# Mixing the score products of one row tile with the maxima products of the other, and banks of two heads for half of the columns

## The reference

```python
att = jnp.einsum('bhtd,bhsd->bhts', q, k) / jnp.sqrt(jnp.asarray(D, x.dtype))
att = att + _alibi_causal_mask(T, H, x.dtype)[None]
att = jax.nn.softmax(att, axis=-1)
y = jnp.einsum('bhts,bhsd->bhtd', att, v)
...
h = jax.nn.silu(jnp.einsum('td,efd->tef', xf, w1))
y = jnp.einsum('tef,edf->ted', h, w2)
```

## Time and profile before

| | us |
|---|---|
| runs (3) | 578.05, 578.42 (median), 579.37 |
| span of the profiled execution | 575.7 |
| second group of heads (168.4 to 260.0) | 91.6 |
| third group of heads (260.0 to 351.6) | 91.6 |
| last group, with tasks (to 393.7), without (to 449.5) | 42.1, 55.8 |
| tile loop and end (449.5 to 575.7) | 126.2 |

### The profile page before, as it was taken

The page is one execution under the profiler, slowest core; times in us unless marked ns, Lnnn a source line. Parts: engine busy times, 40 slices in busy tenths (PEclk is TensorE's granted clock), DMA queues, the critical chain, the costliest instruction groups (busy, mean ns, idle before and its releaser), DMA issues.

```text
span 575.7 us, 15493 instructions
## 1 busy us (share of the span) xinstructions
PE 496.4 (86%) x5876; PEld 264.6 (46%) x5876; DVE 451.9 (79%) x775; ACT 400.9 (70%) x775; POOL 169.9 (30%) x293
## 2 busy tenths in 40 slices
PE   4756878889999999998999999989988999999970
PEld 2422323333243343333334325234433798999970
DVE  3689899989988998998998998995687555554451
ACT  4922366668888888888898887888788656555530
POOL 3310000010103102320034101047057860870864
PEclk9965599999999999999999999999899999999995
DMA  6592111000011450031310000010132222333332
GB/s 158 201 305 65 30 50 36 1 2 4 7 34 34 100 231 3 2 148 32 81 38 3 3 2 2 8 29 9 56 106 63 74 74 61 111 106 91 108 98 66
DMA packets 38263, 37.86 MB, mean 66 GB/s; under 512 B 7088, under 2 KB 33904, under 8 KB 37560
## 3 DMA queue, kind: packets, MB, share of 16 engines
q1 hardware_dynamic: 35808, 32.26, 19.5%
q0 software_dynamic: 2048, 4.20, 2.4%
q10 hardware_dynamic: 336, 0.42, 0.2%
HBM read 20.05 MB, written 16.61 MB: 64 GB/s over the span
## 4 chain that ended last, share of the span: by engine, by line
PE 59%; ACT 9%; DVE 5%; issue 3%; POOL 1%; DMA 1%; ACTq 0%; POOLq 0%; DVEq 0%
PE pv L745 18%; PE b L778 13%; PE b L852 8%; PE b L869 7%; ACT probs L1296 7%; PE b L717 6%; DVE part L1013 3%; PE b L692 3%; ACT raw L1266 1%; POOL raw L1478 1%; PE b L843 1%; PE b L647 1%; PE b L664 1%; ACT rows L1272 0%; DMA raw<-y_scratch,spots 0%
## 5 line engine op out<-in xcount | busy, mean ns | idle before, releaser
L1296 ACT ACTIVATE probs<-b 128x512 f32<-128x512 f32 (+1 forms) x576 | 298.6, 570 | 79.6 <-PE b L692 36.5
L1013 DVE TENSOR_REDUCE part<-b 128x2 f32<-128x1024 f32 (+2 forms) x320 | 327.7, 1061 | 26.8 <-PE b L717 11.8
L745 PE MATMUL pv<-probs,v_cur 128*32 128x256 f32 (+1 forms) x2432 | 176.7, 372 | 0.3 <-ACT probs L1296 0.2
L778 PE MATMUL b<-aug 55*128 55x512 bf16 (+3 forms) x640 | 114.2, 355 | 25.5 <-ACT probs L1296 21.3
L717 PE MATMUL b<-aug 52*128 52x512 bf16 (+3 forms) x640 | 117.1, 366 | 17.4 <-DVE part L1013 15.1
L778 PEld LDWEIGHTS b<-aug 55*128 55x128 bf16 x640 | 37.0, 93 | 137.6 <-ACT probs L1296 131.5
L745 PEld LDWEIGHTS pv<-probs,v_cur 128*32 128x32 f32 x2432 | 50.2, 109 | 68.3 <-issue 40.7
L852 PE MATMUL b<-hTt,inverse 128*128 128x128 f32 x424 | 56.3, 276 | 0.8 <-ACT hTt L1317 0.8
L869 PE MATMUL b<-w2T_sb,hst 128*128 x424 | 56.2, 276 | 0.8 <-ACT hst L1323 0.8
L869 PEld LDWEIGHTS b<-w2T_sb,hst 128*128 128x128 f32 x424 | 51.6, 192 | 1.2 <-issue 1.1
L852 PEld LDWEIGHTS b<-hTt,inverse 128*128 128x128 f32 x424 | 51.5, 192 | 1.0 <-issue 1.0
(11 more groups left out here) (151 smaller groups left out, 374.2 us busy)
## 6 DMA issues: line engine op xcount, KB each, us to landing
xt<-slot_scratch SPq DMA_DIRECT2D x53, 64.0 KB, 1.9
y_scratch<-aug SPq DMA_DIRECT2D x53, 64.0 KB, 1.5
slot_scratch<-slots SPq DMA_DIRECT2D x3, 1024.0 KB, 7.1
aug<-q_scratch SPq DMA_DIRECT2D x6, 384.0 KB
aug<-k_scratch SPq DMA_DIRECT2D x6, 384.0 KB
w2T_sb<-in_w2T SPq DMA_DIRECT2D x1, 2048.0 KB, 7.4
aug<-in_w1T SPq DMA_DIRECT2D x8, 256.0 KB, 2.6
q_scratch<-pieces SPq DMA_DIRECT2D x4, 384.0 KB, 2.6
```

What stands on the lines that cost most here:

```text
L745: return mm(pv[32 * hh:32 * hh + 32, c0:c1], v_cur[:, kb, hh, :], probs[:, step_ % 2, hh, at_:at_ + c1 - c0], start=(kb == 0 and c0 == 0), ...
L778: done.append(mm(pair[half][:, at_:at_ + w], k_aug[g % 2][n, b, kb * P:kb * P + P], q_aug[g % 2][n, b, (j + 1) * CW - w:(j + 1) * CW], sta ...
L1013: ins = nc.vector.tensor_reduce(dst, b1[:, slot:slot + 2, at_:at_ + w], AX.X, ALU.max)
L1296: nc.scalar.activation(probs[:, p % 2, hh, 0:w], b2[:, (n2 - 1) % RING2, 0:w], ACT.Exp).then_inc(exp_done, 1)
```

## The change

The three functions that issue products for a half step become generators that yield after each product, and a new function draws from two of them in turn, one per row tile.

- A bank of `b2` no longer holds one head's scores for all columns of the step, but two heads' (both pairs, one half) for half of the columns, the same half that the value products of that half step number take (`VALUE_PARTS[p][b]`). Each score product has half the columns, and there are twice as many.
- The banks are waited for one at a time, each ahead of its first product.
- The first task of pass 1 of a half step is mixed in: row tile 0 has the scores of half 0 and then the maxima of half 0; row tile 1 has the maxima of half 1 and then the scores of half 1. The two rows of products are issued alternately. Further tasks follow as before, and without a task both score rows alternate.
- Each bank signals ACT by itself. Value products wait only for the exps of their own half of the columns.
- ACT writes an exp's 512 results as two pieces of 256, one per pair.

```diff
-                def mask_out(pair, at_, table, cols):
+                def alternate(low, high):
 
-                    for h, (c0, c1) in enumerate(cols):
-                        for half in range(2):
-                            k = slice(HALF * half, HALF * half + HALF)
-                            ins = mm(pair[half][:, at_ + c0:at_ + c1], identh[k, h, :], table[k, h, c0:c1], start=False, stop=True, skip_group_check=True)
-                    return ins
+                    for _ in zip_longest(low, high):
+                        pass
...
+                def maxima(k, half, opens, closes):
...
+                    if opens:
+                        task_ready(k)
+                    at_ = 0
+                    for r in rs:
+                        w = (r + 1) * P if c == j else CW
+                        t = j * CW + r * P
+                        ins = mm(bank[:, at_:at_ + w], q_aug[buf][n, b, t:t + P], k_aug[buf][n, b, c * CW:c * CW + w], start=True, stop=True)
+                        if c == j:
+                            yield
+                            mask_out(bank, half, at_ + r * P, maskQ, 0, (0, P))
+                            yield
+                            ins = mask_out(bank, half, at_ + r * P, maskQ, 1, (HALF, P))
+                        if closes and r == rs[-1]:
+                            ins.then_inc(s1_ready, 1)
+                        yield
+                        at_ += w
...
+                    pe.wait_ge(exp_done, HG * (NSTEP * g_ + q) + 2 * (b + 1))
                     if b == 0:
-                        pe.wait_ge(exp_done, HG * (NSTEP * g_ + q + 1))
...
-                def scores(p, b):
+                def scores(p, b, half):
...
-                    for half in range(2):
-                        wait_slot(half)
-                    pair = [b2[:, (len(freed) + half) % RING2, :] for half in range(2)]
+                    n = slice(HALF * half, HALF * half + ROWS2)
+                    wait_slot(0)
+                    bank = b2[:, len(freed) % RING2, :]
...
+                    for pair in range(PAIRS):
+                        for kb, _, c0, c1 in parts:
+                            w = c1 - c0
+                            ins = mm(bank[:, at_:at_ + w], k_aug[g % 2][n, pair, kb * P:kb * P + P], q_aug[g % 2][n, pair, j * CW + c0:j * CW + c1], start=True, stop=True)
+                            if c0 == (kb - TPC * j) * P:
+                                yield
+                                mask_out(bank, half, at_, maskT, 0, (0, HALF))
+                                yield
+                                ins = mask_out(bank, half, at_, maskT, 1, (0, P))
+                            if pair == PAIRS - 1 and kb == parts[-1][0]:
+                                ins.then_inc(s2_ready, 1)
+                            yield
+                            at_ += w
+
+                def scores_and_maxima(p, b, upto):
+                    k = at[0]
+                    if k < upto:
+                        alternate(chain(scores(p, b, 0), maxima(k, 0, False, True)), chain(maxima(k, 1, True, False), scores(p, b, 1)))
+                        at[0] += 1
+                    else:
+                        alternate(scores(p, b, 0), scores(p, b, 1))
+                    pass1(upto)
...
-                            scores(p, b)
-                            pass1(min(PLAN[first][p][b], NTASK) if last else PLAN[first][p][b])
+                            scores_and_maxima(p, b, min(PLAN[first][p][b], NTASK) if last else PLAN[first][p][b])
...
-                            nc.scalar.activation(probs[:, p % 2, hh, 0:w], b2[:, (n2 - 1) % RING2, 0:w], ACT.Exp).then_inc(exp_done, 1)
+                            b, half = hh // 2, hh % 2
+                            at_ = VALUE_PARTS[p][b][0][1]
+                            w = sum(c1 - c0 for _, _, c0, c1 in VALUE_PARTS[p][b])
+                            out = probs[:, p % 2, :, at_:at_ + w].rearrange("p (b s) t -> p s b t", s=2)[:, half, :, :]
+                            nc.scalar.activation(out, b2[:, (n2 - 1) % RING2, 0:PAIRS * w].rearrange("p (b t) -> p b t", b=PAIRS), ACT.Exp).then_inc(exp_done, 1)
```

More of the change, by code:

```diff
@@ L13 @@
 from contextlib import ExitStack
+from itertools import chain, zip_longest
 import numpy as np
@@ L685, in group @@
                 at = [0 if first else LEAD]
-                def mask_out(pair, at_, table, cols):
-                    for h, (c0, c1) in enumerate(cols):
-                        for half in range(2):
-                            k = slice(HALF * half, HALF * half + HALF)
-                            ins = mm(pair[half][:, at_ + c0:at_ + c1], identh[k, h, :], table[k, h, c0:c1], start=False, stop=True, skip_group_check=True)
-                    return ins
-                def pass1(upto):
[L696 to L713, removed]
-                            for half in range(2):
[L715 to L722, removed]
@@ new lines, in alternate, with mask_out, task_ready @@
+                def alternate(low, high):
+                    for _ in zip_longest(low, high):
+                        pass
+                def mask_out(bank, half, at_, table, h, cols):
+                    k = slice(HALF * half, HALF * half + HALF)
+                    c0, c1 = cols
+                    return mm(bank[:, at_ + c0:at_ + c1], identh[k, h, :], table[k, h, c0:c1], start=False, stop=True, skip_group_check=True)
+                def task_ready(k):
+                    j = TASKS[k % NTASK][0]
+                    if first and k < NTASK and k == TSTART[j]:
+                        pe.wait_ge(aug0_in[j], 4 * 16)
+                    if first and k == 0:
+                        pe.wait_ge(const_in[0], 6 * 16)
+                    if k == NTASK:
+                        take(pe, aug_in, (4 if first else 8) * 16)
+                        if first:
+                            pe.wait_ge(const_in[1], 6 * 16)
+                    n_task[0] += 1
+                    pe.wait_ge(s1_free, n_task[0])
@@ new lines, in maxima @@
+                def maxima(k, half, opens, closes):
+                    j, c, rs, b = TASKS[k % NTASK]
+                    buf = (g + k // NTASK) % 2
+                    n = slice(HALF * half, HALF * half + ROWS1)
+                    bank = b1[:, 2 * (k % SLOTS) + half, :]
+                    if opens:
[14 more added lines that the diff above has]
+                        at_ += w
@@ L724, in turn @@
+                def pass1(upto):
+                    for k in range(at[0], upto):
+                        alternate(maxima(k, 0, True, False), maxima(k, 1, False, True))
+                    at[0] = max(at[0], upto)
                 def turn(u):
@@ L764, in value_products @@
                         ins.then_inc(pv_done, 1)
-                def scores(p, b):
+                def scores(p, b, half):
                     j, kbs = STEPS[p]
-                    for half in range(2):
-                        wait_slot(half)
-                    pair = [b2[:, (len(freed) + half) % RING2, :] for half in range(2)]
-                    at_ = 0
[L773 to L786, removed]
+                    n = slice(HALF * half, HALF * half + ROWS2)
+                    wait_slot(0)
+                    bank = b2[:, len(freed) % RING2, :]
+                    n_exp[0] += 1
+                    freed.append((exp_done, n_exp[0]))
+                    parts = VALUE_PARTS[p][b]
+                    at_ = 0
+                    for pair in range(PAIRS):
[11 more added lines that the diff above has]
+                            at_ += w
```

1 line of the change is left out of this document (removed).

## The result

The changed kernel takes 563.65 us (median of 4 runs, 561.37 to 565.73) beside 578.23 (576.13 to 579.37) for the kernel before: a ratio of 0.9748, 95% interval 0.9714 to 0.9783, 14.6 us faster. The forecast was 574.2, 4.2 us faster: the right direction, under a third of the size. The profiled span is 561.0 us for 575.7.

The account below looks back on a forecast made before the run. TensorE was taken as the bound, with a small leak at the banks. Second and third group -0.5 us each, first group's end -0.5, last group's start -0.5, tail -2.2: -4.2 in all, 574.2 us, range 559 to 584.

Parts of the forecast that it names:

- What bounds the kernel: Second and third group: TensorE is the bound with a small leak, 6.2 of 91.6 us; VectorE and ScalarE close behind.
- One bank at a time: Each half step's scores: a separate wait per bank removes the stall for two banks at once, 5.8 us a group won.
- Twice the score products: Score products on TensorE: 1216 matmuls for 640, each with half the columns, weight loads hidden, so splitting costs nothing.
- Unequal products side by side: Half steps with masks: products start in program order, so a taken row tile delays the other; 4.6 us a group lost.
- independent tiles: Rival, 15%: no start is held up by the other row tile, so 12.7 us stay won; 561.5 us.
- More waits: Second half's value products and second bank get waits of their own: 0.01 us a half step, 0.7 us a group lost.
- my floor of 1.13: Regular half step: TensorE and VectorE both stand at 1.13 us, against 1.20 in the kernel before.
- The tail: Last group after its maxima: half of the score columns leave the loop of exp and scores; -2.2 us net.
- a switch that costs: Rival, 20%: scores beside a longer product show their 93 ns weight load in 206 half steps; 593 us, half of that 584.
- another wait in its place: Rival, 10%: mixed order couples three engines; half of the 5.8 us comes back, 582 us; a quarter, no change, 578.

Follow-up runs that it names:

- the run tile by tile: The changed kernel, but each half step issues all products of row tile 0 and only then all of row tile 1; 590.63 us, ratio 1.0236.

## Why the prediction was right in direction and a third of the size

- **What bounds the kernel** was right: TensorE with a leak at the banks. The leak is a closed loop, which I described by its stall and not by its parts: exp, release, score, exp, 1.17 and 1.23 us, just above TensorE's 1.11. With the loop open VectorE bounds more than it did: of the chain of work that ended last, its reduces make up 18.7% in the third group (255.6 to 342.9), where they were 6.5% (260.0 to 351.6).
- **One bank at a time** (5.8 us a group) was the cause of most of the gain: with the joint wait the gain is gone (583.83), and split waits and signals in the old order and layout give 12.5 of the 14.0 us measured beside them. I left out that the signal had to be split too; the wait alone gives 3.7. The size was too high: the full change, with the values' wait in it, gives 4.2. I charged 0.09 us to all 69 half steps of the waits view, but where TensorE has masks as well it was late without the wait. A half step of step 13 before, on PE,

```profile
294.91 0.39 PE L778 MATMUL b<-aug 55*128 55x512 bf16 x2
...
295.58 0.64 PE L745 MATMUL pv<-probs,v_cur 128*32 128x256 f32 x8
296.15 0.39 PE L778 MATMUL b<-aug 55*128 55x512 bf16 x2
```

and changed:

```profile
287.21 0.28 PE L795 MATMUL b<-aug 55*128 55x256 bf16 x1
...
287.88 0.64 PE L761 MATMUL pv<-probs,v_cur 128*32 128x256 f32 x8
288.45 0.28 PE L795 MATMUL b<-aug 55*128 55x256 bf16 x1
```

Both take 1.24 us, 0.67 and 0.57, with nothing to win: masks side by side with scores cost no more than before, and there was no stall.
- **Twice the score products** at no cost: right. A full group's TensorE is busy 85.3 us, 0.9 less than before.
- **Unequal products side by side** (4.6 us a group, 12.7 in all) is the step that failed. "One whose row tile is taken holds up those behind it for the free tile" is not so here while at most three wait (302.68 in the run tile by tile, with three left waiting). Taking the term out of the sum gives the rival of independent tiles, 561.5 us; most of the 2.1 us from there to 563.65 go with the overestimate of the leak (0.9 in each full group: 5.1 by that rival's sum, 4.2 measured). I had named steps 13 to 17 and 23 to 25 as the sign, longer by 0.1 to 0.2 us with starts in order, as long as before or shorter with independent tiles: step 17 is 0.12 longer, and the other seven are as long as before or up to 0.10 shorter (13 takes 2.47 both times, 14 2.30 for 2.40). My rows could not decide it: they show only equal products side by side, starting in the order of the program. The rule was my own reading of such rows, and the prediction still gave it most of the chance, and 15% to its opposite.
- **More waits** (0.7 us a group): nothing of it shows; regular half steps came out at 1.11, below my floor of 1.13.
- **The tail** (-2.2): -2.7, near. There ScalarE has become the bound, eight exps in 4.09 us without a gap:

```profile
423.34 4.09 ACT L1325 ACTIVATE probs<-b 128x512 f32<-128x512 f32 x8 [0.20 <-PE b L795]
```

That is 0.50 us each, so a half step needs 1.0 where I had 1.09.
- **The rivals:** a switch that costs is refuted by regular half steps of 1.11; another wait in its place shows at most in steps 17, 26 and 34, 0.12, 0.24 and 0.13 longer, while 18 and 27 behind them are 0.08 and 0.34 shorter; in 26 (at 319.85) maxima wait for VectorE, 0.47 us where it was 0.35.

## What to carry to other kernels

Where two engines pass banks to and fro, draw the loop with every wait and every signal in it, add up its times, and compare with the busiest engine's period: a loop of 1.20 against 1.11 was some 2% of this kernel (12.5 us of 578.0 with nothing but the split wait and signal), and here it opened only with both given per bank: with split signals and a joint wait half steps took 1.18 and 1.24, with a split wait and a joint signal 1.16 and 1.19. Price a stall by the half step's excess over the same work without it, not by the idle time in a waits view: 25.6 us of waiting were left when the stall was gone. And when a term of several us rests on a rule that no row tests, give it a chance of its own in the middle of the sum, and not a footnote.

## What the runs showed of the hardware

Products on different row tiles of TensorE started out of program order (271.90 before 271.93 in the changed kernel), past up to three that waited for the other tile (302.68 in the run tile by tile). With up to eight of one tile issued ahead of the other's, the kernel took 27 us longer (590.63 against 563.65); issued alternately, with 64 to 512 columns side by side, they cost nothing that could be measured (563.65 against 562.25 with equal products side by side where there are masks). Whether a signal on a product issued later covers products of the other tile that were issued before it, no run here tests; the changed kernel has each bank of scores signalled by its own last product.
